# Every second fc1 block's high half of y moves from VectorE to ScalarE, one step behind its SiLU

## What is computed

```
xn  = layernorm(x)
s   = recurrent_memory(xn @ Wq.T, xn @ Wk.T, xn @ Wv.T, M0) @ Wo.T * sigmoid(gate)
h   = layernorm(xn) * gamma + beta
y   = silu(h @ w1 + b1)            # w1: 512 x 2048, dequantised by group of 128 rows
z   = y @ w2 + b2                  # w2: 2048 x 512, dequantised by group of 128 rows
out = x + s * silu(xn + 0.5 * z)
```

## Time and profile before

| what | value |
|---|---|
| median of 3 runs | 1242.57 us (1242.03 to 1242.96) |
| the profiled execution's own time | 1241.93 us |
| its span, first to last instruction | 1240.0 us |
| PE busy | 1184.0 us, 95% |
| DVE busy | 1132.4 us, 91% |
| ACT busy | 913.9 us, 74% |
| POOL busy | 687.8 us, 55% |
| mean granted TensorE clock | 0.986 |

### The profile page before, as it was taken

How to read it: one execution, slowest core, us unless ns; L and a number is a source line. 1 busy time by engine, 2 the same in 40 slices (tenths; PEclk the granted TensorE clock), 3 DMA queues, 4 the chain that set the end, 5 groups by cost and what they waited for, 6 DMA issues and landing times.

```text
span 1240.0 us, 18966 instructions
## 1 busy us (share of the span) xinstructions
PE 1184.0 (95%) x6028; PEld 617.6 (50%) x6028; DVE 1132.4 (91%) x1965; ACT 913.9 (74%) x1590; POOL 687.8 (55%) x780
## 2 busy tenths in 40 slices
PE   2799999999999999999999999999999999999995
PEld 1344555555555555555555555554555555555551
DVE  8799989999898999989998998999989899998888
ACT  6688677777867777777777777777787777778673
POOL 5056727549283663827457373754828276392742
PEclk8799999999999999999999999999999999999998
DMA  9511130402103040120403012040210304010021
GB/s 333 179 45 35 27 77 1 103 1 62 41 14 90 1 103 1 45 58 1 103 1 89 15 32 72 1 102 1 64 39 12 92 1 102 1 51 19 14 56 35
DMA packets 41620, 65.68 MB, mean 53 GB/s; under 512 B 11696, under 2 KB 11952, under 8 KB 41008
## 3 DMA queue, kind: packets, MB, share of 16 engines
q1 hardware_dynamic: 40944, 63.97, 19.3%
q10 hardware_dynamic: 576, 0.47, 0.1%
HBM read 47.59 MB, written 16.81 MB: 52 GB/s over the span
## 4 chain that ended last, share of the span: by engine, by line
PE 80%; DVE 14%; issue 3%; ACT 1%; POOL 1%; DMA 1%; SPq 0%; DVEq 0%; ACTq 0%; POOLq 0%
PE blk L520 30%; PE blk L502 30%; PE side L462 6%; DVE blk L790 5%; PE side L487 4%; PE side L446 3%; DVE g_lo L760 2%; DVE y_split L781 2%; DVE y_split L776 2%; DVE tops L828 1%; PE side L481 1%; PE side L480 1%; PE side L479 1%; PE side L472 1%; PE side L433 1%
## 5 line engine op out<-in xcount | busy, mean ns | idle before, releaser
L790 DVE TENSOR_TENSOR blk<-blk,ratio_rows 128x512 f32<-128x512 f32 x960 | 646.0, 689 | 94.0 <-PE blk L520 86.3
L647 ACT ACTIVATE blk<-blk,ratio 128x512 f32<-128x512 f32 x768 | 508.3, 670 | 242.6 <-PE blk L502 233.1
L520 PE MATMUL blk<-w_sb,y_split 128*128 128x512 f16 x2048 | 608.7, 379 | 10.8 <-DVE y_split L781 8.1
L502 PE MATMUL blk<-h_split,q_sb 128*128 128x512 f16 x2048 | 612.1, 381 | 5.3 <-ACT blk L647 3.1
L520 PEld LDWEIGHTS blk<-w_sb,y_split 128*128 128x128 f16 x2048 | 197.5, 98 | 260.0 <-DVE blk L790 20.6
L502 PEld LDWEIGHTS blk<-h_split,q_sb 128*128 128x128 f16 x2048 | 192.9, 98 | 218.2 <-issue 36.8
L654 ACT ACTIVATE y_full<-blk,par,last 128x512 f32<-128x512 f32 x256 | 201.7, 788 | 54.6 <-PE blk L502 54.2
L1089 POOL CAST h_split<-h_full 128x512 f16<-128x512 f32 x64 | 41.4, 647 | 328.1 <-ACT h_full L602 328.1
L781 DVE SCALAR_TENSOR_TENSOR y_split<-y_full,up,y_split 128x512 f16<-128x512 f32 x256 | 217.2, 849 | 0.0
L776 DVE TENSOR_SCALAR y_split<-y_full,up 128x512 f16<-128x512 f32 x256 | 155.7, 608 | 0.0
L1133 POOL TENSOR_TENSOR z_rows<-z_rows,s_rows 128x512 f32<-128x512 f32 x62 | 89.1, 1437 | 52.6 <-ACT z_rows L673 52.6
(11 more groups left out here) (153 smaller groups left out, 1095.3 us busy)
## 6 DMA issues: line engine op xcount, KB each, us to landing
xt<-in_x SPq DMA_DIRECT2D x64, 256.0 KB, 4.7
x_again<-in_x SPq DMA_DIRECT2D x256, 64.0 KB, 1.9
out<-z_rows SPq DMA_DIRECT2D x250, 64.0 KB, 1.7
w_sb<-in_q SPq DMA_DIRECT2D x4, 1024.0 KB, 13.8
ratio_rows<-ratio_dram SPq DMA_DIRECT2D x4, 1024.0 KB, 8.1
y_split<-in_q SPq DMA_DIRECT2D x1, 1024.0 KB, 9.9
h_split<-in_q SPq DMA_DIRECT2D x1, 1024.0 KB, 12.2
z_rows<-in_q SPq DMA_DIRECT2D x1, 1024.0 KB, 14.3
```

Of the source, the lines that this page charges most:

```text
L502: mm = pe.matmul(blk[J % 2][:], q1_sb[:, g, j // 4, w, j % 4 * P:(j % 4 + 1) * P], a[:, c % 2, g, :], start=(g == 0 and n == 0), stop=(g = ...
L520: mm = pe.matmul(blk2[:, i, :], y[:, J % Y_RING, rows], w2_sb[:, j, part, :], start=(j == 0 and n == 0), stop=(j == FB - 1 and n == len(te ...
L647: act.activation(blk[J % 2][:], blk[J % 2][:], ACT.Copy, scale=ratio1[:, at:at + 1]).then_inc(blk_scaled, 1)
L790: dve.tensor_tensor(blk2[:, i, :], blk2[:, i, :], ratio2_rows[:, j, :], ALU.mult).then_inc(blk2_scaled, 1)
```

## The change

For odd blocks J the high half is no longer written by DVE's `tensor_scalar` but by an ACT `activation` (Copy, with the per-partition scale `up_y`). It stands in ACT's loop one step behind the SiLU, right behind that step's `rescale`: at steps 4, 12, 20, 28, 36, 44, 52 and 60. Even blocks stay on DVE, and every low half does. A new semaphore counts the odd high halves for `y_low`; another tells ACT once that `up_y` exists, by a 128x1 copy that DVE makes before its loop.

```
+            def odd_y_high(J):
+                wait(act, blk2_done, NT * (J - Y_RING + 1))
+                if J == 1:
+                    act.wait_ge(y_scale, 1)
+                act.wait_ge(silu_done, J + 1)
+                act.activation(y_hi[:, J % Y_RING, :], y_full[:, J % 2, :], ACT.Copy, scale=up_y
+                               ).then_inc(y_hi_odd_done, 1)
...
                         rescale(*at)
                     else:
                         silu(at[0])
+                if (at := fc1_step(G - YHIGH_LAG) if G >= YHIGH_LAG else None) and at[1] == KC - 1 and at[0] % 2:
+                    odd_y_high(at[0])
...
             def y_low(J):
-                dve.wait_ge(y_hi_done, J + 1)
+                if J % 2:
+                    dve.wait_ge(y_hi_odd_done, J // 2 + 1)
+                else:
+                    dve.wait_ge(y_hi_done, J // 2 + 1)
...
+            dve.tensor_copy(branch_end[:], up_y).then_inc(y_scale, 1)
+
             for G in range(SLOTS):
...
-                if (at := fc1_step(G - YHIGH_LAG) if G >= YHIGH_LAG else None) and at[1] == KC - 1:
+                if (at := fc1_step(G - YHIGH_LAG) if G >= YHIGH_LAG else None) and at[1] == KC - 1 and at[0] % 2 == 0:
                     y_high(at[0])
```

More of the change, by code:

```diff
@@ L280, in build @@
         silu_done = sem("silu_done")
-        y_hi_done = sem("y_hi_done")
+        y_hi_done, y_hi_odd_done = sem("y_hi_done"), sem("y_hi_odd_done")
         y_lo_done = sem("y_lo_done")
+        y_scale = sem("y_scale")
         blk2_done = sem("blk2_done")
```

## The result

| | before | changed |
|---|---|---|
| median | 1242.38 us (4 runs) | 1274.98 us (4 runs, 1274.82 to 1275.27) |
| ratio | 1 | 1.0263, 95% interval 1.0246 to 1.0279 |
| span of the profiled execution | 1240.0 us | 1273.3 us |

The change costs 32.6 us; 33.7 were forecast, and 1276 for 1274.98.

The account below looks back on a forecast made before the run. PE bounds the kernel, at ACT's pace at some steps. Steps 4, 20, 28 25.1, turn 7.6, chunk 0 1.4, 128x1 copy 0.1, tail -0.5: 33.7 us, forecast 1276 us, range 1260 to 1286.

Parts of the forecast that it names:

- the slack of 0.19: Between ACT's rescale of step 5 and PE's step 7: 0.24 - 0.05 = 0.19 us to spare.
- Steps 7 and 24: PE's fc1 pairs delayed by the operations moved at steps 4 and 20: losses of 0.43 and 0.62 us a chunk.
- d: Price of one moved operation, how much later ACT moves on: 0.62 us taken, bounds 0.47 and 0.72.
- Step 32: PE's fc1 pair behind ACT's SiLU of step 30, delayed by the operation at step 28: loss 0.62 us.
- The turn: Operations at steps 52 and 60, up to the next chunk's step 1: 0.54 us, 2d - 0.70, 14 times, 7.6 us.
- Lateness takes that in: At step 60, PE's 0.19 us wait for DVE's g_lo is absorbed, leaving PE 0.29 late instead of 0.48.
- Here DVE gives something back: At step 0 the low half comes 0.40 us earlier, so the fc2 pair is 0.18 late, limited by ACT.
- Chunk 0 and the tail: Chunk 0 loses 1.4 us, the 128x1 copy ahead of the loop 0.1; the tail counts as -0.5.
- ACT's idle time hides the operation: Rival: ACT's 233 us of waiting hide it and DVE's relief counts, 1236 us; chance 0.04.
- only the turn pays: Rival: losses at steps 4, 20 and 28 are made up by removed later waits; 8 us, 1250; chance 0.08.
- the operation does not overlap: Rival: the semaphore wait keeps the new operation from overlapping on both sides, d = 0.82; 49 us, 1292; chance 0.08.
- nothing changes: Rival: no change within 0.2%, as gain and loss meet; needs d near 0.18; chance 0.02.

Follow-up runs that it names:

- two swaps of neighbours: Transposes at 46, 52, 56, 60 on the kernel before, plus DVE's low half ahead of step 61's scaling and ACT's h_full behind step 63's rescale: 1234.98 us, 0.9945.
- a better spread of the transposes: Kernel before with the next chunk's transposes at steps 46, 52, 56 and 60 instead of 52, 54, 57 and 60: 1238.93 us, 0.9973.
- the later gates: Kernel before with transposes at 46, 50, 54, 58 and the gate's SiLUs at 15, 25, 26, 27 instead of 17, 19, 21, 29: 1281.14 us, 1.0312.

## Why the prediction was right

**The place of the bound.** The step from the busy shares to the timeline was the one that mattered: DVE at 91% was worth 7.6 us in all (the run without odd high halves), and ACT at 74% set PE's pace at steps 24, 32, 59 and 0 of the changed kernel and, once the slack of 0.19 was used up, at step 7. Steps 7 and 24 cost what the prediction said to 0.01 us, and the run with only steps 12, 36 and 44 shows that the slack there was real.

**The price.** d was 0.62 as taken, from the row of the one float32 copy with a scale; the operation took 0.71 us for 0.72. By the Trainium skill, "ScalarE: Activation LUTs", section What ACT_TABLE_LOAD costs, the estimate from its figures is 0.613; the start-to-start time of 0.62 in the rows of step 4 above agrees. The run without the scale operand shows what that operand costs: 712 - 621 = 91 ns.

**Step 32**: 0.49 for 0.62. ACT costs PE what was forecast (0.42 us at step 31, 0.18 at step 32). The missing 0.12 is a side effect that the sum did not have: PE's matmul with `wo_sb` at step 27 waited for DVE's `mem_t` in the kernel before, and with the change it does not. The waits tables of before and of the changed kernel:

```profile
PEld side L487 <- DVE mem_t L770: 5.8, 15, 1.0
```

```profile
PEld side L488 <- DVE mem_t L781: 0.5, 1, 0.5
```

The wait goes with the high half of step 20: it is gone too where only steps 20 and 28 are moved and where nobody makes the odd high halves, and it stays where steps 12, 36 and 44 are moved (6.4 us, 16 times) and where DVE keeps all its high halves (5.7 us, 15 times).

**The turn**: 0.62 us (0.47 + 0.41 - 0.26) for 0.54. Two steps of the working failed. "Lateness takes that in" did not happen: the transpose of step 60 still starts late for g_lo, 721.71 - 720.65 = 1.06 us between the pairs, as before. DVE was late by as much as PE, and the rows say why. Before (DVE, then POOL):

```profile
698.85 0.91 DVE L776 TENSOR_SCALAR y_split<-y_full,up 128x512 f16<-128x512 f32 x1
```

```profile
698.33 1.16 POOL L1093 TENSOR_TENSOR h_split<-h_full,h_split 128x512 f16<-128x512 f32 x1
```

and with the change:

```profile
717.25 1.38 DVE L787 TENSOR_SCALAR y_split<-y_full,up 128x512 f16<-128x512 f32 x1
```

```profile
717.19 1.16 POOL L1109 TENSOR_TENSOR h_split<-h_full,h_split 128x512 f16<-128x512 f32 x1
```

POOL's operation stands behind a cast that waits for ACT's `h_full`, and so was 0.47 late with ACT (717.19 - 698.33 = 18.86 against the 18.39 of step 32). DVE's high half was not late (18.40) but now met the whole of POOL's operation, took 0.47 us longer and handed that on to g_lo. This error did not reach the sum, though: the prediction took PE's steps 0 and 1 from ACT's ends, 0.87 late, whatever PE had lost at step 61. There the size was off. ACT's last operations of the turn started only 0.81 late but took longer and ended 0.93 late; its queue is unbroken now, where it paused for 0.06 us ahead of the rescale of step 61 before. The SiLU of step 62, 0.78 us in the earlier trace rows:

```profile
723.74 0.91 ACT L655 ACTIVATE y_full<-blk,par,last 128x512 f32<-128x512 f32 x1
```

So PE's step 0 came 0.88 late for 0.80 and step 1 0.62 for 0.54.

**Where DVE gives back.** "Here DVE gives something back" was incomplete. It gives back at step 0, and besides keeps the low half of step 24 off the path, 0.42 us a chunk that the sum never saw, because it did not ask how late the low halves would come with ACT loaded and the odd high halves still on DVE. It did not hurt the forecast, as the changed kernel has that relief; it would have, had I costed the load alone.

**Chunk 0 and the tail.** The fc1 pair of step 1 of chunk 1 starts at 119.18 before and 120.99 changed: 1.8 us for 1.5 taken. Of these 0.4 stand ahead of the loop, where kernels with the same work ahead of it differ by as much (step 0 of chunk 0 at 29.88 before and at 30.58 in the run with no odd high halves), so the 0.1 for the 128x1 copy can't be seen. The same pair of chunk 15 is 31.9 us late and the end 33.3: 1.4 us for 1.67 - 0.5 = 1.2.

**How the total came out.** Against the sum, step 32 was 15 x 0.13 = 2.0 us cheaper, and the turn 14 x 0.08 = 1.1, chunk 0 0.3 and the end 0.2 us dearer. That the total is so close, 33.3 us in the profiled execution for 33.7, is in part luck: errors of opposite sign met. The mechanism is borne out by the single steps, not by the total.

**What the profile should have shown.** The new group, its 0.71 us and the pace of 0.62 are there, and so are the chunk's 2.15 us and the fc1 pairs directly behind ACT's ends. Three sayings were off. DVE's busy time fell by 15.5 us and not by 50 to 60, and so its idle time grew by 49 us and not by more than 80; both are explained below. And the waits of PE and PEld for ACT's rescale and SiLU grew from 49.6 to 146.3 us, by 97 and not by 30, where PE lost 33. Most of them are idle time of the weight loads, which runs while the matmul before is still at work, and is no measure of lost time.

**The rivals.** That ACT's idle time hides the operation falls by the result, and by the run with steps 20 and 28 alone; that only the turn pays, by the same run; that the operation does not overlap, by the 0.62 us in the trace; that nothing changes, by the result.

## What to carry to other kernels

Where a hand-made order runs several engines in step, a busy share says nothing about room: put the end of the feeding operation beside the start of the one it feeds, step by step, and the price of an added operation is its start-to-start time less the slack at that step. Moving work from a busier engine to an idler one pays only at steps where the idler one has slack and the busier one is waited for, and here these steps did not coincide. Try the order within an engine first: here two swaps of neighbours brought 4 us and a better spread of the transposes 3.4, and no move between engines brought anything.

## What was not expected of the hardware

DVE's operations on SBUF alone stretch beside POOL's. In the changed kernel (DVE, then POOL):

```profile
678.67 1.28 DVE L804 TENSOR_TENSOR blk<-blk,ratio_rows 128x512 f32<-128x512 f32 x2
679.87 1.51 DVE L787 TENSOR_SCALAR y_split<-y_full,up 128x512 f16<-128x512 f32 x1
681.30 0.69 DVE L804 TENSOR_TENSOR blk<-blk,ratio_rows 128x512 f32<-128x512 f32 x1
681.90 1.15 DVE L795 SCALAR_TENSOR_TENSOR y_split<-y_full,up,y_split 128x512 f16<-128x512 f32 x1
```

```profile
679.83 1.26 POOL L1149 TENSOR_TENSOR z_rows<-z_rows,s_rows 128x512 f32<-128x512 f32 x1
681.17 1.33 POOL L1152 TENSOR_TENSOR z_rows<-z_rows,x_again 128x512 f32<-128x512 f32 x1
```

A high half that takes 0.48 us by the median took 1.51, a low half 1.15 instead of 0.74, each ending some 0.3 to 0.6 us after the POOL operation that was running; the multiplication between them, which reads PSUM, kept its 0.69. By the Trainium skill, "SBUF — State Buffer", section SBUF: two separate sides, DVE and GpSimd share a port pair, which a GpSimd instruction, or a DVE instruction in a 2-port mode or with two SBUF inputs, holds for its whole length while the other waits; the rows agree in kind, and no run here shows which mode a high half ran in.

The change made such meetings dearer. The 128 high halves of the odd blocks, which it took off DVE, had 68.5 us before, 535 ns each. Those of the even blocks, which stayed, had 87.3 us before and 106.9 after, 682 and 835 ns each, and the low halves 217.2 before and 232.5 after. In sum the durations of all of DVE's operations fell by 32 us only. Its busy time fell by 15.5, as neighbours overlap by some 0.08 us at either end and busy time counts that once. Which DVE operation meets a POOL operation is set by the phase of two queues, so every shift of POOL's work, as with the later gates, is a change of DVE's times too.
